# Second layer's attention: projections as row halves in two phases, last turns in bank pair B, value products at the end of the step

## The reference, cut to what matters

```
PAD = -30000.0
q, k, v = jnp.einsum('bsx,xMnd->Mbnsd', x, qkv)
s = x.shape[1]
a = jnp.einsum('bnsd,bntd->bnst', q, k) * q.shape[-1] ** (-0.5)
cum = jnp.cumsum(rpe_bias[:, :s], axis=-1)
rel = jnp.arange(s)[:, None] - jnp.arange(s)[None, :]
bias = jnp.where(rel >= 0, cum[:, jnp.clip(rel, 0)], PAD)
a = jax.nn.softmax(a + bias, axis=-1)
mix = jnp.einsum('bnst,bntd->bnsd', a, v)
return jnp.einsum('bnsd,ndx->bsx', mix, out_w)
```

## Times and profile before

| | us |
|---|---|
| median of 3 runs | 2346.9 (2346.76 to 2347.49) |
| profiled execution, its own time | 2347.72 |
| its span in the trace | 2345.9 |
| TensorE busy | 2102.0 (90% of the span) |
| VectorE busy | 1630.3 (69%) |
| ScalarE busy | 1325.4 (56%) |
| GpSimd busy | 945.8 (40%) |

### The profile page before, as it was taken

The page is one execution under the profiler, slowest core; times in us unless marked ns, Lnnn a source line. Parts: engine busy times, 40 slices in busy tenths (PEclk is TensorE's granted clock), DMA queues, the critical chain, the costliest instruction groups (busy, mean ns, idle before and its releaser), DMA issues. The chain is left out here.

```text
span 2345.9 us, 51161 instructions
## 1 busy us (share of the span) xinstructions
PE 2102.0 (90%) x19252; PEld 1298.8 (55%) x19252; DVE 1630.3 (69%) x4801; ACT 1325.4 (56%) x2688; POOL 945.8 (40%) x1175
## 2 busy tenths in 40 slices
PE   4679998998999999999999796899999985899886
PEld 2447776996677777777776665233333334333333
DVE  7666663775666676666665553999989946589896
ACT  2247775655777777777777242276767672323322
POOL 2036765664668734665343032111111110054462
PEclk9689998999999999999999698699999996899998
DMA  6311112214011100000000053111211101000000
GB/s 178 109 59 37 37 36 70 68 37 147 20 35 20 35 2 20 2 20 2 2 2 2 13 177 117 30 40 40 49 37 37 37 7 37 0 0 0 9 9 18
DMA packets 77908, 93.78 MB, mean 40 GB/s; under 512 B 10145, under 2 KB 56242, under 8 KB 76002
## 3 DMA queue, kind: packets, MB, share of 16 engines
q1 hardware_dynamic: 64178, 77.23, 11.0%
q0 software_dynamic: 13488, 13.28, 2.8%
HBM read 54.55 MB, written 35.53 MB: 38 GB/s over the span
## 5 line engine op out<-in xcount | busy, mean ns | idle before, releaser
L1069 ACT ACTIVATE WA<-a_E 128x1024 f32<-128x1024 f32 (+1 forms) x320 | 282.8, 939 | 128.2 <-PE a_E L1002 70.2
L982 PE MATMUL a_S<-a_KS,a_QS 54*128 54x512 bf16 (+3 forms) x768 | 202.3, 354 | 37.4 <-DVE a_mx L1104 26.4
L455 POOL TENSOR_SCALAR WA<-WA,a1b_rinv 128x1024 f32<-128x1024 f32 (+3 forms) x192 | 147.8, 818 | 159.5 <-DVE a1b_rinv L754 159.4
L455 POOL TENSOR_SCALAR XR<-XR,a1b_rinv 128x768 f32<-128x768 f32 (+3 forms) x192 | 145.1, 784 | 155.9 <-DVE a1b_rinv L754 155.6
L572 PE MATMUL a1b_O<-a1b_PT,WA 128*64 128x128 f32 x3072 | 188.9, 276 | 0.0
L572 PEld LDWEIGHTS a1b_O<-a1b_PT,WA 128*64 128x64 f32 x3072 | 165.8, 137 | 6.5
L982 PEld LDWEIGHTS a_S<-a_KS,a_QS 54*128 54x128 bf16 x768 | 53.5, 94 | 205.0 <-DVE a_mx L1104 102.1
L1020 PE MATMUL a_O<-WA,V 128*9 128x512 f32 (+3 forms) x1536 | 159.9, 504 | 0.1
L1102 DVE TENSOR_REDUCE a_mx<-a_S 128x1 f32<-128x512 f32 x256 | 156.8, 681 | 1.7 <-PE a_S L982 1.7
L535 PE MATMUL a1b_B<-a1b_Kf,a1b_Qf 64*128 64x512 f32 (+2 forms) x768 | 153.4, 471 | 1.3 <-DVE a1b_firstmax L741 1.1
L670 ACT ACTIVATE WA<-WA,a1b_nmax 128x1024 f32<-128x1024 f32 (+3 forms) x192 | 150.3, 787 | 1.3 <-DVE a1b_nmax L741 1.3
(11 more groups left out here) (497 smaller groups left out, 5400.6 us busy)
## 6 DMA issues: line engine op xcount, KB each, us to landing
WA<-in_w SPq DMA_DIRECT2D x8, 1024.0 KB, 9.0
a_QS<-qstack SPq DMA_DIRECT2D x32, 216.0 KB
a_KS<-kstack SPq DMA_DIRECT2D x32, 216.0 KB
a1b_tb<-tab SPq DMA_DIRECT2D x12, 512.0 KB, 4.7
qstack<-f_parts SPq DMA_DIRECT2D x24, 256.0 KB, 3.8
kstack<-f_parts SPq DMA_DIRECT2D x24, 256.0 KB, 3.9
f_slots<-f1r_zrows SPq DMA_DIRECT2D x9, 516.0 KB
f1t_xs<-f_slots SPq DMA_DIRECT2D x9, 516.0 KB, 7.2
```

What stands on the lines that cost most here:

```text
L455: pool.tensor_scalar(v, v, rinv[:, e, u, part:part + 1], 1.0, ALU.mult, ALU.mult).then_inc(n_sb, 1)
L982: ins = pe.matmul(pS[(at + half) % SB][:, lo:lo + n], QS[s][ROW[half], pair, i * P:(i + 1) * P], KS[s][ROW[half], pair, c * CH:c * CH + n] ...
L1069: act.activation(PT[q % NP][:, :, 0:w], pE[q % 2][:, :, 0:w], ACT.Exp).then_inc(e_sb, 1)
```

## The change

- `BY_ACT` goes from 4 to 3: ScalarE no longer copies turn 2.
- Bank pair B becomes one tensor of two banks, and turn 2 writes into columns 256 to 383 of both of its banks instead of C. VectorE reads both halves in one copy (`copy_last`), and takes the second reciprocal ahead of it.
- The two pieces of other work are no longer done on the whole array one after the other. `beside(it, e, 0)` stands ahead of scores 2, `beside(it, e, 1)` behind turn 2. In each, for four blocks of 128 columns, one row half serves bank P and the other bank C1; in the second phase the halves are swapped and add to what the first left.
- The wait for ScalarE's copies out of C now stands ahead of the first `beside`, since that writes C1.
- The values of step-1 move from behind turn 1 to the end of the step.

```diff
-    BY_ACT, BY_DVE = 4, 2
+    BY_ACT, BY_DVE = 3, 2
...
-    pA, pB, pC = ([ph.ps(f"{n}{h}") for h in range(2)] for n in "ABC")
+    pA, pC = ([ph.ps(f"{n}{h}") for h in range(2)] for n in "AC")
+    pair = ph.ps("B", (P, HG, CH))
+    pB = [pair[:, h, :] for h in range(2)]
     pS = (pB, pA, pB)
-    pT = (pA, pC, pC)
+    pT = (pA, pC, [bank[:, 2 * P:3 * P] for bank in pB])
     pO = ph.ps("O")
...
+    pc_ps = ph.sem("pcps")
...
+            def project_rows(bank, p, kind, half, t, k, order):
+                rows, b = slice(k * QH, (k + 1) * QH), p % B
+                out, i = bank[:, t * P:(t + 1) * P], half * CT + t
+                xnt = XNT[rows, b, 1 + i * P:1 + (i + 1) * P]
+                lhs, rhs = (xnt, wv[rows, :]) if kind == 2 else ((wq, wk)[kind][rows, :], xnt)
+                ins = pe.matmul(out, lhs, rhs, start=order + t == 0, stop=order + t == CT)
+                if t == CT - 1 and order == 1:
+                    ins.then_inc((q_ps, k_ps, v_ps)[kind], 1)
+                return ins
+
+            def output_rows(bank, p, j, t, k, order):
+                rows, i = slice(k * QH, (k + 1) * QH), TILES[j][t]
+                ins = pe.matmul(bank[:, t * P:(t + 1) * P], mU[p % 2][rows, i * P:(i + 1) * P], wo[rows, :],
+                                start=order + t == 0, stop=order + t == CT)
+                if t == CT - 1 and order == 1:
+                    ins.then_inc(y_ps, 1)
+                return ins
...
             def output(bank, p, j):
-                if p < 0:
-                    return
-                if p % B == 0 and j == 0:
-                    pe.wait_ge(wo_ok, p // B + 1)
-                pe.wait_ge(o_sb, p * 2 + j + 2)
                 for t, i in enumerate(TILES[j]):
                     ins = pe.matmul(bank[:, t * P:(t + 1) * P], mU[p % 2][:, i * P:(i + 1) * P], wo[:, :], start=True, stop=True)
                 ins.then_inc(y_ps, 1)
+
+            def beside(it, e, order):
+                step = it * E + e
+                if order:
+                    pe.wait_ge(pc_ps, begun[step + 1])
+                for t in range(CT):
+                    last_p, last_c = None, None
+                    if e == 0 and it + 1 < IT:
+                        last_p = project_rows(pP, it + 1, 0, 1, t, order, order)
+                        last_c = project_rows(pC[1], it + 1, 1, 0, t, 1 - order, order)
+                    elif e == 1 and it + 1 < IT:
+                        last_p = project_rows(pP, it + 1, 1, 1, t, order, order)
+                        last_c = project_rows(pC[1], it + 1, 2, 0, t, 1 - order, order)
+                    elif e == 2:
+                        if it + 1 < IT:
+                            last_p = project_rows(pP, it + 1, 2, 1, t, order, order)
+                        if it:
+                            last_c = output_rows(pC[1], it - 1, 0, t, 1 - order, order)
+                    elif e == 3:
+                        if it:
+                            last_p = output_rows(pP, it - 1, 1, t, order, order)
+                        if it + 2 < IT:
+                            last_c = project_rows(pC[1], it + 2, 0, 0, t, 1 - order, order)
+                    for ins in (last_p, last_c):
+                        if ins and order == 0 and t == CT - 1:
+                            ins.then_inc(pc_ps, 1)
...
+                if n == 0 and step:
+                    pe.wait_ge(s_sb, step * R)
+                    if step > 2:
+                        pe.wait_ge(t_sb_a, (step - 2) * BY_ACT)
+                        pe.wait_ge(t_sb_d, (step - 2) * BY_DVE)
...
+                elif n == 2:
+                    pe.wait_ge(s_sb, step * R + HG)
                 for u in range(HG):
...
-                elif r == 2:
-                    pe.wait_ge(t_sb_a, step * BY_ACT + 3)
-                elif step:
-                    pe.wait_ge(t_sb_a, step * BY_ACT)
+                elif r == 2 and step + 2 >= ALL:
+                    pe.wait_ge(s_sb, ALL * R)
                     pe.wait_ge(t_sb_d, step * BY_DVE)
...
                     turn(step, 1)
-                    if step:
-                        values(step - 1)
                     scores(step + 2, 1)
-                    scores(step + 2, 2)
-                    turn(step, 2)
+                    pe.wait_ge(t_sb_a, step * BY_ACT + 3)
                     if e == 0 and it + 1 < IT:
...
-                        project(pP, it + 1, 0, 1)
...
+                    beside(it, e, 0)
+                    scores(step + 2, 2)
+                    turn(step, 2)
+                    beside(it, e, 1)
+                    if step:
+                        values(step - 1)
...
                     copy(step, 1)
                     exponential(step + 1, 1, 0)
                     exponential(step + 1, 0, 1)
-                    copy(step, 2)
                     exponential(step + 1, 1, 1)
                     if e == 0:
...
-            def copy(step, r):
-                dve.wait_ge(t_ps, step * 3 + r + 1)
-                dve.tensor_copy(*half(step, r, 1)).then_inc(t_sb_d, 1)
+            def copy_first(step):
+                dve.wait_ge(t_ps, step * 3 + 1)
+                dve.tensor_copy(*half(step, 0, 1)).then_inc(t_sb_d, 1)
+
+            def copy_last(step):
+                dve.wait_ge(t_ps, step * 3 + 3)
+                dve.tensor_copy(turned_last[step % 2].rearrange("p (j h q) -> p h j q", h=2, q=QH),
+                                pair[:, :, 2 * P:3 * P].rearrange("p h (j q) -> p h j q", q=QH)).then_inc(t_sb_d, 1)
...
                     order = wide_first((step + 2) % E)
-                    copy(step, 0)
+                    copy_first(step)
                     for u in range(HG):
                         bias(step + 2, order[0], u)
                     inverse(step + 1, 0)
-                    bias(step + 2, order[1], 0)
-                    copy(step, 2)
-                    bias(step + 2, order[1], 1)
+                    for u in range(HG):
+                        bias(step + 2, order[1], u)
+                    inverse(step + 1, 1)
+                    copy_last(step)
                     for u in range(HG):
                         bias(step + 2, order[2], u)
-                    inverse(step + 1, 1)
```

More of the change, by code:

```diff
@@ L391, in attention @@
         ph.sem(n) for n in ("tps", "tsba", "tsbd", "pvps", "osb", "yps", "xsb"))
+    pc_ps = ph.sem("pcps")
+    begun = [0]
+    for it in range(IT):
+        for n in range(E):
+            begun.append(begun[-1] + (2 * (it + 1 < IT), 2 * (it + 1 < IT),
+                                      (it + 1 < IT) + (it > 0), (it > 0) + (it + 2 < IT))[n])
     def tile_of(e, c):
@@ L420, in half @@
     def half(step, r, h):
-        v = turned_first[step % 2][r] if r < 2 else turned_last[step % 2]
-        return (v.rearrange("p (j h q) -> p j h q", h=2, q=QH)[:, :, h, :],
-                pT[r][h][:, 0:(TT if r < 2 else 2) * QH].rearrange("p (j q) -> p j q", q=QH))
+        return (turned_first[step % 2][r].rearrange("p (j h q) -> p j h q", h=2, q=QH)[:, :, h, :],
+                pT[r][h].rearrange("p (j q) -> p j q", q=QH))
     def groups(ap, h):
@@ L490, in project @@
             def project(bank, p, kind, half):
-                if p >= IT:
-                    return
                 b = p % B
@@ L523, in scores @@
                 lo, hi = keys(e, c)
+                if n == 0 and step:
[3 more added lines that the diff above has]
+                        pe.wait_ge(t_sb_d, (step - 2) * BY_DVE)
+                elif n == 1 and step >= 2:
+                    pe.wait_ge(t_sb_a, (step - 2) * BY_ACT + 1)
+                    pe.wait_ge(t_sb_d, (step - 2) * BY_DVE + 1)
+                elif n == 1 and step:
+                    pe.wait_ge(s_sb, 2 * HG)
+                elif n == 2:
+                    pe.wait_ge(s_sb, step * R + HG)
                 for u in range(HG):
                     head = slice(u * D, (u + 1) * D)
[L526 to L534, removed]
                     pe.matmul(pS[n][u][:, 0:hi - lo], Qf[head, s, i * P:(i + 1) * P], Kf[head, s, lo:hi],
@@ L629, in _ @@
-                    pe.wait_ge(t_sb_d, (step + 1) * BY_DVE)
-                    if e == 0 and it + 1 < IT:
-                        if b == B - 1:
-                            pe.wait_ge(wk_ok, g + 2)
-                        project(pC[1], it + 1, 1, 0)
-                    elif e == 1 and it + 1 < IT:
                         if b == B - 1:
                             pe.wait_ge(wv_ok, g + 2)
-                        project(pC[1], it + 1, 2, 0)
-                    elif e == 2 and it:
-                        output(pC[1], it - 1, 0)
-                    elif e == 3 and it + 2 < IT:
-                        if b == B - 2:
-                            pe.wait_ge(wq_ok, g + 2)
-                        project(pC[1], it + 2, 0, 0)
+                    elif e == 2:
+                        if it + 1 < IT:
+                            pe.wait_ge(k_sb, it * 2 + 4)
+                        if it:
```

(9 more changed lines are left out.)

11 lines of the change are left out of this document (3 added, 8 removed).

## The result

The changed kernel takes 2435.4 us (median of 4 runs, 2433.1 to 2438.2), the kernel before 2347.2 beside it: a ratio of 1.0372, with a 95% interval of 1.0354 to 1.0390, or 88 us more where 26 were forecast and 2391 was the upper end of the range. The direction and the main mechanism were right; the size was not. Of the 62 us that are missing, 45 turned out to hang on the chip that the kernel runs on. The kernel before takes 2346 to 2350 on either.

A forecast was written before the change was run, and what follows sets the result against it. TensorE's own list was taken as the bound: 0.43 us a step saved, 0.65 lost waiting for C. 31 items x 0.90 is 28 us, less 2: 2347.7 + 26 = 2373.7 profiled, 2373 as median; range 2357 to 2391.

The forecast's parts named there:

- The bound and the sign: Changed stage: TensorE's list bounds the step, saves 0.43 us, but idles 0.65 on average; slower by more than 4.7 us, 0.86.
- Rival A: Phase one: copies of C do not hold it up, only mode changes count; 55 us less, 2292; 9% with partial gains.
- additions for mode changes: TensorE's step before the change: extra time where the array's shape changes, said to come to 0.71 us for four changes.
- The starts of phase one: First projection phase, waiting for ScalarE's copies out of C: starts 3.45, 3.35, 3.35, 3.55 us into the step (e = 0 to 3).
- The release: From the end of a producer to TensorE's first product: 0.11 us, with bounds 0.04 and 0.2.
- Phase one at 0.86: First row-half projection phase, ahead of scores 2: 8 passes at 0.1075 us, both halves side by side, no addition.
- Phase two: Second row-half projection phase, behind turn 2: 0.86 + 0.05 + 0.09 us, the additions for following a turn and leaving.
- rival C: Projection phases: row halves take turns, 218 us more, some 2590, 3%; mild form, passes of 0.12, near 2398, 7%.
- Take off 2 for steps of the join: Steps of the join: GpSimd's lateness no longer shows there, so 2 us come off the 28 us total.
- Rival D: Whole stage: the pauses lower TensorE's clock; no size given, chance 1%.
- Theory S: From the experiments, not the prediction: the place of GpSimd's indirect transfers in the step decides whether TensorE's signals are held back.

The follow-up runs named there:

- e5: Changed kernel, but VectorE instead of ScalarE takes the second copy out of C: 2340.0 us, ratio 0.9968 to the kernel before.
- e1: Changed kernel, but with the value products of step - 1 again between turn 1 and scores 1: 2325.5 us, ratio 0.9905 to the kernel before.
- e17: Kernel of e1, but TensorE waits only for the half of K it reads and VectorE takes Q before adding the output: 2304.1 us, ratio 0.9825.
- e9: The changed kernel again, unaltered, on another chip, a quiet one: 2390.3 us, ratio 1.0180 to the kernel before.

## Why the prediction was half right

**The bound and the sign: right.** TensorE was the bound, its own list did get shorter, and the wait for ScalarE's copies out of C more than ate it up. e5 shows that wait as the cause (50 us with one copy moved off ScalarE), e1 shows that the place of the value products makes it (69 us). Rival A, that only the mode changes count, is near what one gets without the wait: 2292 was said, the kernel of e1 gives 2321 on quiet chips, and e17, with two more waits taken away, 2304 and steps of 7.29 where the list came to 7.20. (The additions for mode changes that the prediction lists come to 0.76, not 0.71; no later sum uses them.)

**The starts of phase one: right.** 3.45, 3.35, 3.35, 3.55 were forecast, 3.39, 3.29, 3.29, 3.50 measured (from the item above and its next three steps). The release took 0.05, inside the bounds of 0.04 and 0.2.

**Phase one at 0.86: the term that was too small.** It is 0.99 where TensorE has waited before it, and 0.89 in e1 where it has not. I had booked no addition there, since it follows row-half work, and had not asked what the first pass after a pause costs: 0.1 a step, 13 us over both calls. Phase two, at 1.04 with entering and leaving, was close to the 1.00 booked. The row halves did work side by side (passes of 0.11), so rival C does not apply, mild form included.

**"Take off 2 for steps of the join": wrong sign.** The steps of the join that were 0.1 to 0.4 longer before are indeed as long as the others now, some 1.3 us in all. But in step 43 of `a1b` ScalarE computes a root for the join; in the first profile after:

```profile
958.82 1.28 ACT L1659 ACT_TABLE_LOAD   x1
960.12 0.32 ACT L1659 ACTIVATE WA<-WA,eps 128x32 f32<-128x32 f32 x1
...
960.93 1.28 ACT L714 ACT_TABLE_LOAD   x1
...
963.84 0.58 ACT L721 COPY a1b_PT<-a1b_C 128x512 f32<-128x512 f32 x1
```

The two table loads of 1.28 each now stand in the chain to phase one, and the step takes 12.6 us; before it took 8.4. (The Trainium skill, ScalarE: Activation LUTs, What ACT_TABLE_LOAD costs, calls the load a real instruction of ScalarE of about 1283 ns; the trace agrees with 1.28. The drain of about 1380 ns that the page adds does not show here: the root starts 0.02 after the first load's end.) What the loads cost the kernel is the wait behind them. I had called everything on ScalarE ahead of the copies unchanged and looked at one item to say so.

**The sum on a quiet chip.** Of the 42 us between e9 and its kernel before, `a1b` has 32.3 (757.1 between first and last turn 0 against 724.8): 95 steps at the forecast 0.225 are 21.4, the first passes 10.5, step 43 4, the rest of the stage -3.6. The other 10 lie in the first call and at the ends of both. 2390 is 17 above the forecast and inside its range.

**The moved transfers: the step that was left out.** The change shifts GpSimd's two indirect transfers of a step from beside the value products to beside turn 0 and its readers, and every DMA that a moved step issues had to be counted. I gave them no sentence, so that the prediction put at nothing what became the largest missing term: the copies out of A, taken to start 0.76 after the step's start in every step, start up to 2.4 after it near the transfers on a holding chip, which is 45 of the 62 us missing. (In `a1b` the first transfer of a step started 1.6 us after turn 0 before, and 0.5 to 0.7 ahead of it now.) The trace before could not have shown the 45 us, since that profile was of a quiet chip; but it did show the transfers at 0.95 to 1.21 us each (1.55 to 1.62 where they add), and a bound for "something of theirs reaches turn 0, scores 0 or turn 1", about 1 us in each of the 64 steps that have them, would have put the upper end near 2440. Rival D, at 1%, came true in a small way in three of those steps and in step 43.

**What is shown and what is not.** Shown: on two of the five chips whose traces tell (the first profile after makes it one more occasion) TensorE's signals are late near indirect transfers, in every kernel there that has them, the kernel before included; plain transfers, which are also shorter, end it; the time lost depends on what covers them. Not shown: why these chips, whether it is the chip or something else that was constant over a group of runs, whether the kind or the length of the transfers matters, and what holds the signal. Theory S is refuted as to whether signals are late; how much the place of the transfers changes the size of the effect was not measured.

## What to carry to other kernels

Long work without a signal, like these value products, is a cover for everything that is late around it; before moving it, list what lies beside it, other engines' DMAs included, and price each as if it were bare. A wait that opens on the bounding engine costs the wait and, here, 0.1 us more for the slow first pass behind it. And a result from another chip is compared only with the unchanged kernel and the changed one run there.

## What the runs showed of the hardware that was not expected

- TensorE's completion signals can arrive 0.1 to 1.7 us late during and up to a microsecond after an indirect transfer of GpSimd, on some chips and not on others; of VectorE, ScalarE and GpSimd 304 of 355 signals in the same stretches of the first profile were recorded within 0.02 us of their instruction's end, and none 0.02 to 0.4 us late; for the other 51 the trace has no record at that time (in e9 it has one for all 458), so whether they were sent on time stays open. TensorE's delayed signals then come 0.04 us apart (644.62, 644.66 and 644.71 in the step above), as two undelayed ones that are due together do.
- The rows' data start to move 0.6 to 0.7 us after the instruction's recorded end. (The Trainium skill, Perfetto Trace Analysis, DMA Instruction — SWDGE, says that this end is that of the descriptors' generation and not of the movement; the trace agrees.)
- The first pass of row-half products after a pause takes 0.21 us instead of 0.11, at a granted clock of 1.00 (phase one of the first profile and of e5). Why was not tested.
- A product of 64 rows with new weights for every 128 columns, in both row halves, keeps the pace of 0.11 us a pass in both.
